# A chunked selective scan: the product with C takes columns 0 to 15 of a chunk, and the products lie with the channel block innermost

## The chip, the cores and the metric

The kernel runs on one core of one Trainium2 chip. The metric is the device time of one execution in microseconds. The engines are TensorE (PE, with its weight loads as PEld), VectorE (DVE), ScalarE (ACT), GpSimd (POOL) and the queue of SyncE (SP), which issues the DMAs.

## The reference, cut to what matters

The network has four residual layers on x of shape (8, 1024, 256): a selective scan block, a mixture of 16 experts, an attention layer and the same mixture again. The change touches the scan. For every channel e (512) and state n (16), and for every time t of 1024:

```
dA = exp(clip(dt[..., None] * A, -10.0, 0.0))
h = dA * h + dt[..., None] * bt[:, None, :] * xt[..., None]
scale = where(|h| > 10.0, 10.0 / |h|, 1)        # norm over n
h = where(t % 16 == 15, h * scale, h)
y = einsum('bn,ben->be', ct, h) + D_param * xt
```

So at each 16th step the state is bounded by its norm, and the bounded state both goes on and enters y. After it y is multiplied by silu(z), projected, normalised and added.

## The kernel before, in words

A tile is 128 consecutive times of one batch entry; there are 64 tiles, and a tile is eight chunks of 16 times (CH = 16, NC = 8). Channels lie on the 128 partitions, in four blocks (EB = 4), with N = 16 states each, so a chunk of the state is 128 partitions by 64 rows of 17 columns: hb[c % 2], whose column 0 is the bounded state that comes in and whose columns 1 to 16 are the times of the chunk.

Per chunk: POOL writes B*u into columns 1 to 16 (inputs, L364). ACT writes the decays exp(dt*A) to PSUM (exponentials, L426). DVE runs the recurrence in place (scan, L980). Then comes the bounding chain: ACT squares column 16 (L432), DVE sums over the states (reduce, L988), ACT makes the factor with a logarithm and an exponential (norms, L438 and L441), and DVE writes the bounded state twice (bound): L997 into column 0 of the other buffer, from which the next scan starts (semaphore st0), and L999 into column 16 of its own buffer (semaphore hs). POOL multiplies columns 1 to 16 by C into prod (product, L356) when hs has come. PE sums the products over n in quarters of a tile (sum_states, L700, 16 transposing matmuls by the identity), ACT copies the sums (L447), PE turns them back into the bank YP, where D*x has been laid before by skip (L741), and DVE multiplies YP by silu(z) (L1154).

The order of each engine is written out in its own step function and is fixed: loops over c from 0 to 7 in which stages of several tiles are interleaved. The letters of the stages are L, F, G (the head of later tiles: norm, projections, convolution, dt, u, decays), S (the scan), B (the rest of the tile before), X and Y (router and experts of tiles further back). Engines meet only by semaphores. On POOL iteration c has product(c-1), inputs(c+1) and, in some chunks, one extra multiply: u in 1 (L373), sz in 4 (L377), xcv in 5 (L380), x1b in 7 (L384). DVE has in each iteration the scan, two expert sums (L1071) for PE's expert pairs (L734), the reduction, other work of the tile, and the bounding.

prod is two buffers of [N, EB, 32 times], one for each quarter in turn. cbc and bbc hold half a tile of C and B, spread over the partitions by DMA; SP reloads them when prodp or bt says that their last reader is done. After the last tile merged runs the attention and the second mixture, 64 slots to a batch entry; twelve pairs of the last two tiles' first mixture are done in the slots LATE of its first batch, all in the one bank G0 (GM); G is (G0, G1), and G1 is also YT, the bank of the state sums.

Of the kernel before, what the change touches and what calls it, by code (L numbers as in the profile page):

```python
# [8 lines left out]
P = 128  # L9
# [20 lines left out]
def build(nc, dram, out):  # L30
# [3 lines left out]
    with ctx:  # L34
# [39 lines left out]
        prod = [sb(f"prod{k}", [P, N, EB, QT]) for k in range(2)]  # L74
# [54 lines left out]
        w_a = prod[0][:].rearrange("p a b c -> p (a b c)").rearrange("p (w k d) -> p w k d", w=4, k=KD)  # L129
        mats = prod[1][:].rearrange("p a b c -> p (a b c)").rearrange("p (m c) -> p m c", c=P)  # L130
# [123 lines left out]
        def chunk_product(c):  # L254

            t0, tq = (c % HC) * CH, (c % QC) * CH
            return (prod[(c // QC) % 2][:].rearrange("p n e t -> p e n t")[:, :, :, tq:tq + CH],
                    hb[c % 2][:].rearrange("p (e n) s -> p e n s", e=EB)[:, :, :, 1:SL],
                    cbc[c // HC][:, :, t0:t0 + CH].rearrange("p (e n) s -> p e n s", e=1).broadcast_to([P, EB, N, CH]))
# [6 lines left out]
        def _(sp):  # L266
# [19 lines left out]
            def step(i, k, stages):  # L286
# [12 lines left out]
                if "G" in stages:  # L299
# [7 lines left out]
                    products_done(sp, i, HC - 1)  # L307
# [38 lines left out]
        def _(g):  # L346
            head_start(g, (M, pool_m))
            TT = nc.gpsimd.tensor_tensor

            def product(i, k, c):  # L350

                g.wait_ge(M["hs"], AHEAD + i * NC + c + 1)
                g.wait_ge(M["cc0" if c < HC else "cc1"], AHEAD + (i + 1) * 16)
                g.wait_ge(M["y"], AHEAD + i * 4 + c // QC - 1)
                dst, states, cc = chunk_product(c)
                TT(dst, states, cc, ALU.mult).then_inc(M["prodp"], 1)  # L356

            def inputs(i, k, c):
# [3 lines left out]
                products_done(g, i if c >= 2 else i - 1, (c - 2) % NC)  # L362
                t0, half = c * CH, c // HC
# [22 lines left out]
            def step(i, k, stages):  # L386
                for c in range(NC):
                    if c == 0 and "B" in stages:
                        product(i - 1, 1 - k, NC - 1)
                    if c > 0 and "S" in stages:  # L390
                        product(i, k, c - 1)
                    if c < NC - 1 and "S" in stages:
                        inputs(i, k, c + 1)
                    extra(i, k, c, stages)
                if "G" in stages:
                    inputs(i + 1, 1 - k, 0)
# [5 lines left out]
        def _(a):  # L402
# [31 lines left out]
            def norms(i, c):  # L434
# [5 lines left out]
                a.wait_ge(M["hs"], AHEAD + q)  # L440
# [248 lines left out]
        def _(pe):  # L689
# [4 lines left out]
            def sum_states(i, h):  # L694

                products_done(pe, i, (h + 1) * QC - 1)
                if h % 2 == 0:
                    pe.wait_ge(M["yt"], AHEAD + i * 2 + h // 2)
                for n in range(N):
                    last = mm(YT[:, h * P:(h + 1) * P], prod[h % 2][:, n, :, :].rearrange("p e t -> p (e t)"), ident[:],  # L700
# [37 lines left out]
            def skip(i, k):  # L738

                for e in range(EB):  # L740
                    mm(YP[:].rearrange("p (h e t) -> p e h t", h=4, e=EB)[:, e, :, :], ddp[:, e, :],  # L741
                       xcv[k][:, e, :].rearrange("p (h t) -> p h t", h=4), start=(e == 0), stop=False)
# [188 lines left out]
            def slot(b, t, p):  # L931
                n = (b - 1) * NT + t
                if b == 0 and t * (X // 2) + p in LATE:
                    m, q = late_pair(t * (X // 2) + p)
                    experts_mm(m, m % 2, q, q + 1, GM)
                if b > 0:
                    experts_mm(n + NTILES, n % 2, p, p + 1, G4 if b == NB else G, fresh=(b in (1, NB) and t == 0))
# [13 lines left out]
        def _(v):  # L951
# [38 lines left out]
            def bound(i, c, top=1.0):  # L990
# [3 lines left out]
                v.wait_ge(M["ne"], AHEAD + q + 1)  # L994
                last = cur[:, :, CH:SL].rearrange("p (e n) s -> p e (n s)", e=EB)
# [3 lines left out]
                STT(last, factor, 1.0, last, ALU.min, ALU.mult).then_inc(M["hs"], 1)  # L999
# [94 lines left out]
            def step(i, k, stages):  # L1094
# [54 lines left out]
                if B:  # L1149
# [4 lines left out]
                    TT(yg[:].rearrange("p e (h t) -> p h e t", h=4), YP[:].rearrange("p (h e t) -> p h e t", h=4, e=EB),  # L1154
                       sz[1 - k][:].rearrange("p e (h t) -> p h e t", h=4), ALU.mult).then_inc(M["yg"], 1)
# [294 lines left out]
```

## Time and profile before

| | us |
|---|---|
| median of 3 runs (lowest, highest) | 4447.61 (4446.76, 4454.78) |
| the profiled execution | 4455.33 |
| its span | 4453.3 |
| PE busy | 3967.3 (89%) |
| DVE busy | 3625.9 (81%) |
| ACT busy | 3121.9 (70%) |
| POOL busy | 2589.8 (58%) |

The scan stage takes the first 27 of 40 equal slices of the span; POOL works in it alone, and after it PE is busy at 90% or more of nearly every slice. Busy time counts instructions, not waits, and start and end of neighbours on one engine overlap by some 0.05 to 0.1 us.

### The profile page before, as it was taken

What the parts mean: (1) busy time and instruction counts of PE and PEld (TensorE: products, weight loads), DVE (VectorE), ACT (ScalarE), POOL (GpSimd) and SP (SyncE); (2) the same over time, 40 slices, a digit from 0 to 9 for tenths busy, and PEclk for the clock granted to TensorE, in tenths of its full rate; (3) what the DMA queues carried; (4) which work ended last, traced back from release to release, by engine and by line L of the source; (5) the groups of instructions that cost most, each with busy time, mean ns of one, the idle gap of its engine ahead of it and who ended that gap; (6) DMA issues with size and microseconds to landing.
All of it is one profiled execution on the core that took longest, in us unless ns stands there. A gap on an engine that the chain in (4) does not pass through costs nothing.

```text
span 4453.3 us, 72570 instructions
## 1 busy us (share of the span) xinstructions
PE 3967.3 (89%) x18752; PEld 2605.9 (59%) x18752; DVE 3625.9 (81%) x9566; ACT 3121.9 (70%) x9232; POOL 2589.8 (58%) x1284
## 2 busy tenths in 40 slices
PE   6788888888888888888888888868999999999999
PEld 5666666666666666666666666634455454454454
DVE  4899999999999999999999999864657666666677
ACT  6899999999999999999999999834333333333321
POOL 4898989889888888898988988840000000000000
PEclk8899999999999999999999999989999999999999
DMA  3111111111111111111111111110000000000000
GB/s 112 53 54 55 54 59 50 59 54 58 54 58 54 58 54 54 54 53 60 50 60 53 58 54 58 53 37 22 7 16 7 16 16 6 16 16 6 7 8 10
DMA packets 91556, 187.43 MB, mean 42 GB/s; under 512 B 16160, under 2 KB 58016, under 8 KB 90912
## 3 DMA queue, kind: packets, MB, share of 16 engines
q1 hardware_dynamic: 91424, 185.92, 13.0%
q8 instruction: 52, 0.85, 0.1%
q14 instruction: 80, 0.66, 0.0%
HBM read 168.05 MB, written 17.83 MB: 42 GB/s over the span
## 4 chain that ended last, share of the span: by engine, by line
PE 39%; issue 22%; POOL 18%; DVE 17%; ACT 3%; DVEq 1%; POOLq 1%; SPq 0%; DMA 0%; ACTq 0%
PE ps L734 21%; POOL prod L356 11%; PE ps L839 5%; DVE macc L1071 4%; POOL hb L364 3%; PE ps L874 3%; PE ps L856 2%; POOL xcv L380 2%; ACT zr L417 2%; DVE sg L1254 2%; POOL u L373 1%; PE ps L833 1%; PE ps L789 1%; PE ps_dA L874 1%; DVE xin L1185 1%
## 5 line engine op out<-in xcount | busy, mean ns | idle before, releaser
L734 PE MATMUL ps<-w_x,mxT 128*128 128x512 f32 x4096 | 1962.3, 607 | 114.6 <-DVE macc L1071 114.6
L1071 DVE SCALAR_TENSOR_TENSOR macc<-ps,gate,macc 128x256 f32<-128x256 f32 x2048 | 978.7, 478 | 492.6 <-PE ps L734 408.8
L980 DVE TENSOR_TENSOR_SCAN hb<-ps_dA,hb 128x1088 f32<-128x1088 f32 x512 | 1240.5, 2423 | 90.1 <-POOL hb L364 77.7
L356 POOL TENSOR_TENSOR prod<-hb,cbc 128x1024 f32<-128x1024 f32 x512 | 1122.5, 2192 | 234.3 <-DVE hb L999 234.0
L364 POOL TENSOR_TENSOR hb<-u,bbc 128x1024 f32<-128x1024 f32 x512 | 1203.1, 2350 | 75.1 <-POOL prod L356 70.9
L417 ACT ACTIVATE zr<-dt,aneg 128x128 f32<-128x128 f32 x4096 | 1239.8, 387 | 0.0
L734 PEld LDWEIGHTS ps<-w_x,mxT 128*128 128x128 f32 x4096 | 736.0, 194 | 819.6 <-issue 601.4
L700 PE MATMUL ps<-ident,prod 128*128 128x128 f32 x4096 | 554.6, 295 | 12.8 <-POOL prod L356 9.6
L700 PEld LDWEIGHTS ps<-ident,prod 128*128 128x128 f32 x4096 | 513.0, 153 | 25.3 <-POOL prod L356 22.5
L426 ACT ACTIVATE ps_dA<-zr 128x1024 f32<-128x1024 f32 x512 | 518.2, 1012 | 0.0
L477 ACT ACTIVATE ex<-lgt,ms 128x16 f32<-128x16 f32 x128 | 39.1, 305 | 357.9 <-DVE ms L1019 357.9
L432 ACT ACTIVATE sq<-hb 128x64 f32<-128x64 f32 x512 | 158.3, 309 | 174.2 <-DVE hb L980 172.0
L811 PEld LDWEIGHTS ps<-xin,dcw 128*128 128x128 f32 x2048 | 247.3, 198 | 40.7 <-DVE xin L1185 25.3
L811 PE MATMUL ps<-xin,dcw 128*128 128x128 f32 x2048 | 248.4, 281 | 11.0 <-DVE xin L1185 11.0
L839 PE MATMUL ps<-xcv,w_dt 128*128 128x128 f32 x2048 | 253.2, 283 | 0.0
L839 PEld LDWEIGHTS ps<-xcv,w_dt 128*128 128x128 f32 x2048 | 241.0, 197 | 13.5 <-issue 13.5
L773 PE MATMUL ps<-ident,xn 128*128 128x128 f32 x128 | 31.8, 336 | 157.3 <-ACT xn L520 157.3
L833 PE MATMUL ps<-xcv,w_xp 128*32 128x128 f32 x512 | 70.9, 284 | 103.4 <-POOL xcv L380 103.4
L789 PE MATMUL ps<-xnT,w_in 128*128 128x128 f32 x1024 | 150.6, 310 | 3.9 <-ACT xnT L542 3.9
L789 PEld LDWEIGHTS ps<-xnT,w_in 128*128 128x128 f32 x1024 | 145.8, 227 | 4.7 <-ACT xnT L542 3.4
L997 DVE SCALAR_TENSOR_TENSOR hb<-ps_dA,hb 128x64 f32<-128x64 f32 x480 | 125.9, 262 | 24.9 <-ACT ps_dA L441 21.9
L833 PEld LDWEIGHTS ps<-xcv,w_xp 128*32 128x32 f32 x512 | 52.2, 112 | 154.0 <-POOL xcv L380 150.3
(197 smaller groups left out, 5102.8 us busy)
## 6 DMA issues: line engine op xcount, KB each, us to landing
bbc<-bcd SPq DMA_DIRECT2D x128, 512.0 KB, 3.7
cbc<-bcd SPq DMA_DIRECT2D x128, 512.0 KB, 3.8
xt<-in_x SPq DMA_DIRECT2D x128, 128.0 KB, 3.7
x2d<-macc SPq DMA_DIRECT2D x64, 128.0 KB, 1.7
out_dram<-macc SPq DMA_DIRECT2D x64, 128.0 KB, 1.7
w_x<-in_w_x SPq DMA_DIRECT2D x1, 4096.0 KB, 14.8
hb<-x2d SPq DMA_DIRECT2D x32, 128.0 KB, 2.3
sz<-x2d SPq DMA_DIRECT2D x16, 128.0 KB, 2.2
```

Source lines behind the costliest of these rows:

```text
L356: TT(dst, states, cc, ALU.mult).then_inc(M["prodp"], 1)
L364: TT(hb[c % 2][:].rearrange("p (e n) s -> p e n s", e=EB)[:, :, :, 1:SL], u[k][:, :, t0:t0 + CH].rearrange("p e (n s) -> p e n s", n=1).br ...
L417: last = act(zr[k][:, s, :], dt[:, s // N, :], ACT.Relu, bias=10.0, scale=aneg[:, s:s + 1])
L426: act(dA3[:, :, 1:SL], zr[k][:, :, c * CH:(c + 1) * CH], ACT.Exp, bias=-10.0).then_inc(M["dA"], 1)
L700: last = mm(YT[:, h * P:(h + 1) * P], prod[h % 2][:, n, :, :].rearrange("p e t -> p (e t)"), ident[:], start=(h % 2 == 0 and n == 0), stop ...
L734: last = mm(banks[p % len(banks)][:], mxT[k][:, j, :], w_x[:, j, p * 512:(p + 1) * 512], start=(j == 0), stop=(j == KD - 1))
L789: last = mm(F0[:, m * P:(m + 1) * P], w_in[:, j, m * P:(m + 1) * P], xnT[:, j, :], start=(j == 0), stop=(j == KD - 1))
L811: last = mm(F0[:, e * P:(e + 1) * P], dcw[:, e * TAPS + t, :], xin[:, e, t:t + P], start=(t == 0), stop=(t == TAPS - 1))
L839: last = mm(F0[:, m * P:(m + 1) * P], w_dt[:, e, m * P:(m + 1) * P], xcv[k][:, e, :], start=(e == 0), stop=(e == EB - 1))
L874: last = mm(QUAD[s % 4][:], w_a[:, w, kk, j * P:(j + 1) * P], xTa[:, kk, g * TG:(g + 1) * TG], start=(kk == 0), stop=(kk == KD - 1))
L980: V.tensor_tensor_scan(states, dA, states, 0.0, ALU.mult, ALU.add).then_inc(M["scan"], 1)
L1071: STT(macc[k][:], banks[(e // 2) % len(banks)][:, (e % 2) * D:(e % 2 + 1) * D], gate[k][:, e:e + 1], macc[k][:], ALU.mult, ALU.add).then_i ...
```

## The change

The product takes columns 0 to 15 of a chunk instead of 1 to 16. Column 0 is the bounded state of the chunk before, so the column that needs the second bounding form is read from the next chunk's buffer instead. The product waits for the scan; only the last column of a tile (last_product) waits for the second form, which is left in chunk 7 alone. In chunk 0 the product takes columns 1 to 15, and in chunk 4 it is cut in two, since column 0 belongs to the first half of C. On POOL iteration c now has product(c), the extra, and inputs(c+2). These inputs wait for the squares and the first form of chunk c, and the first form waits for product c-1, which reads the column that it writes. prod is one buffer of [N, 64 times, EB]; a quarter's sums wait for product 2, 4, 6 or the last one. The late expert pairs alternate between G0 and G1.

```
-        prod = [sb(f"prod{k}", [P, N, EB, QT]) for k in range(2)]
+        prod = sb("prod", [P, N, HT, EB])
...
+        QUARTER_ENDS = (2, 4, 6, 7)
+        def states_product(c, s0, s1):
+            t0 = c * CH + s0 - 1
+            half, at, w = t0 // HT, t0 % HT, s1 - s0
+            return (prod[:].rearrange("p n t e -> p e n t")[:, :, :, at:at + w],
+                    hb[c % 2][:].rearrange("p (e n) s -> p e n s", e=EB)[:, :, :, s0:s1],
+                    cbc[half][:, :, at:at + w].rearrange("p (e n) s -> p e n s", e=1).broadcast_to([P, EB, N, w]))
...                                                          # SP
-                    products_done(sp, i, HC - 1)
+                    products_done(sp, i, HC)
...                                                          # POOL, product
-                g.wait_ge(M["hs"], AHEAD + i * NC + c + 1)
-                g.wait_ge(M["cc0" if c < HC else "cc1"], AHEAD + (i + 1) * 16)
+                g.wait_ge(M["scan"], AHEAD + i * NC + c + 1)
                 g.wait_ge(M["y"], AHEAD + i * 4 + c // QC - 1)
-                dst, states, cc = chunk_product(c)
-                TT(dst, states, cc, ALU.mult).then_inc(M["prodp"], 1)
+                if c == 0:
+                    g.wait_ge(M["cc0"], AHEAD + (i + 1) * 16)
+                    multiply(c, 1, CH).then_inc(M["prodp"], 1)
+                elif c == HC:
+                    multiply(c, 0, 1)
+                    g.wait_ge(M["cc1"], AHEAD + (i + 1) * 16)
+                    multiply(c, 1, CH).then_inc(M["prodp"], 1)
+                elif c < NC - 1:
+                    multiply(c, 0, CH).then_inc(M["prodp"], 1)
+                else:
+                    multiply(c, 0, CH)
+            def last_product(i):
+                g.wait_ge(M["hs"], AHEAD + i + 1)
+                multiply(NC - 1, CH, SL).then_inc(M["prodp"], 1)
...                                                          # POOL, inputs
+                g.wait_ge(M["sq"], AHEAD + i * NC + c - 1)
+                g.wait_ge(M["st0"], AHEAD + i * NC + c - 1)
...                                                          # POOL, step
-                    if c == 0 and "B" in stages:
-                        product(i - 1, 1 - k, NC - 1)
-                    if c > 0 and "S" in stages:
-                        product(i, k, c - 1)
-                    if c < NC - 1 and "S" in stages:
-                        inputs(i, k, c + 1)
+                    if "S" in stages:
+                        product(i, k, c)
                     extra(i, k, c, stages)
-                if "G" in stages:
-                    inputs(i + 1, 1 - k, 0)
+                    if c == NC - 1 and "S" in stages:
+                        last_product(i)
+                    if c < NC - 2 and "S" in stages:
+                        inputs(i, k, c + 2)
+                    if c >= NC - 2 and "G" in stages:
+                        inputs(i + 1, 1 - k, c + 2 - NC)
...                                                          # ACT, norms
-                a.wait_ge(M["hs"], AHEAD + q)
+                a.wait_ge(M["st0"], AHEAD + q)
+                if c == 0:
+                    a.wait_ge(M["hs"], AHEAD + i)
...                                                          # PE
-                products_done(pe, i, (h + 1) * QC - 1)
+                products_done(pe, i, QUARTER_ENDS[h])
-                    last = mm(YT[:, h * P:(h + 1) * P], prod[h % 2][:, n, :, :].rearrange("p e t -> p (e t)"), ident[:],
+                    last = mm(YT[:, h * P:(h + 1) * P], prod[:, n, h % 2 * QT:(h % 2 + 1) * QT, :].rearrange("p t e -> p (t e)"), ident[:],
-                    mm(YP[:].rearrange("p (h e t) -> p e h t", h=4, e=EB)[:, e, :, :], ddp[:, e, :],
-                       xcv[k][:, e, :].rearrange("p (h t) -> p h t", h=4), start=(e == 0), stop=False)
+                    mm(YP[:].rearrange("p (t e) -> p e t", e=EB)[:, e, :], ddp[:, e, :], xcv[k][:, e, :], start=(e == 0),
+                       stop=False)
...
-                    experts_mm(m, m % 2, q, q + 1, GM)
+                    if t * (X // 2) + p == LATE[0]:
+                        pe.wait_ge(R["ac"], AHEAD + m * (X + 1) + 2 * q + 1)
+                        pe.wait_ge(M["yt"], AHEAD + NTILES * 2)
+                    experts_mm(m, m % 2, q, q + 1, G)
...                                                          # DVE, bound
+                products_done(v, i, c - 1)
                 STT(nxt[:, :, 0:1].rearrange("p (e n) s -> p e (n s)", e=EB), factor, top, last, ALU.min, ALU.mult)\
                     .then_inc(M["st0"], 1)
-                STT(last, factor, 1.0, last, ALU.min, ALU.mult).then_inc(M["hs"], 1)
+                if c == NC - 1:
+                    STT(last, factor, 1.0, last, ALU.min, ALU.mult).then_inc(M["hs"], 1)
...
-                    TT(yg[:].rearrange("p e (h t) -> p h e t", h=4), YP[:].rearrange("p (h e t) -> p h e t", h=4, e=EB),
-                       sz[1 - k][:].rearrange("p e (h t) -> p h e t", h=4), ALU.mult).then_inc(M["yg"], 1)
+                    TT(yg[:], YP[:].rearrange("p (t e) -> p e t", e=EB), sz[1 - k][:], ALU.mult).then_inc(M["yg"], 1)
...
-                    expert_sums(m, m % 2, 2 * q, 2 * q + 2, GM)
+                    expert_sums(m, m % 2, 2 * q, 2 * q + 2, G)
```

## Rows read from the trace of the kernel before

**Rows 1.** Windows: busy us and count of each engine in 400 to 2800 us.
```profile
400.00:2800.00 2400.00, 2098.10 (x12091) 1562.34 (x12090) 2222.74 (x5363) 2192.03 (x6684) 2146.72 (x1061) 0.96 0.17 56
```

**Rows 2.** POOL by line, whole run: busy us, mean ns, idle before and its releasers.
```profile
L364 POOL TENSOR_TENSOR hb<-u,bbc 128x1024 f32<-128x1024 f32 x512 | 1203.1, 2350 | 75.1 <-POOL prod L356 70.9 <-PE ps L700 0.2
L356 POOL TENSOR_TENSOR prod<-hb,cbc 128x1024 f32<-128x1024 f32 x512 | 1122.5, 2192 | 234.3 <-DVE hb L999 234.0
L377 POOL TENSOR_TENSOR sz<-zt,sg 128x512 f32<-128x512 f32 x64 | 81.8, 1278 | 6.3 <-ACT sg L564 6.3
L384 POOL TENSOR_TENSOR x1b<-oo,xt 128x256 f32<-128x256 f32 x64 | 47.2, 738 | 13.9 <-DVE oo L1193 13.9
```

**Rows 3.** Timeline of DVE, chunks 0 to 5: start us, us, instruction, idle before.
```profile
1415.55 2.42 DVE L980 TENSOR_TENSOR_SCAN hb<-ps_dA,hb 128x1088 f32<-128x1088 f32 x1 [0.17 <-issue]
...
1420.63 0.26 DVE L997 SCALAR_TENSOR_TENSOR hb<-ps_dA,hb 128x64 f32<-128x64 f32 x1
...
1421.03 2.42 DVE L980 TENSOR_TENSOR_SCAN hb<-ps_dA,hb 128x1088 f32<-128x1088 f32 x1
...
1425.46 0.27 DVE L997 SCALAR_TENSOR_TENSOR hb<-ps_dA,hb 128x64 f32<-128x64 f32 x1 [0.22 <-ACT ps_dA L441]
...
1426.05 2.42 DVE L980 TENSOR_TENSOR_SCAN hb<-ps_dA,hb 128x1088 f32<-128x1088 f32 x1
...
1429.81 0.42 DVE L1163 TENSOR_TENSOR oo<-oo,ps 128x256 f32<-128x256 f32 x1 [0.31 <-PE ps L796]
1430.26 0.43 DVE L1165 BATCH_NORM_STATS2 st<-oo 128x6 f32<-128x256 f32 x1
...
1431.13 0.26 DVE L997 SCALAR_TENSOR_TENSOR hb<-ps_dA,hb 128x64 f32<-128x64 f32 x1
...
1431.95 2.42 DVE L980 TENSOR_TENSOR_SCAN hb<-ps_dA,hb 128x1088 f32<-128x1088 f32 x1 [0.40 <-POOL hb L364]
...
1438.00 2.42 DVE L980 TENSOR_TENSOR_SCAN hb<-ps_dA,hb 128x1088 f32<-128x1088 f32 x1
...
1442.98 2.42 DVE L980 TENSOR_TENSOR_SCAN hb<-ps_dA,hb 128x1088 f32<-128x1088 f32 x1
```

**Rows 4.** The same timeline, from the end of chunk 5 to the next tile.
```profile
1448.09 0.25 DVE L997 SCALAR_TENSOR_TENSOR hb<-ps_dA,hb 128x64 f32<-128x64 f32 x1
...
1448.84 2.42 DVE L980 TENSOR_TENSOR_SCAN hb<-ps_dA,hb 128x1088 f32<-128x1088 f32 x1 [0.33 <-POOL hb L364]
...
1454.04 0.21 DVE L1245 TENSOR_SCALAR sc<-mv,sc 128x1 f32<-128x1 f32 x1
1454.72 2.42 DVE L980 TENSOR_TENSOR_SCAN hb<-ps_dA,hb 128x1088 f32<-128x1088 f32 x1 [0.47 <-POOL hb L364]
...
1460.33 2.42 DVE L980 TENSOR_TENSOR_SCAN hb<-ps_dA,hb 128x1088 f32<-128x1088 f32 x1
```

**Rows 5.** Timeline of ACT: the squares of chunks 4 and 5.
```profile
1440.45 0.32 ACT L432 ACTIVATE sq<-hb 128x64 f32<-128x64 f32 x1 [0.93 <-DVE hb L980]
...
1446.01 0.30 ACT L432 ACTIVATE sq<-hb 128x64 f32<-128x64 f32 x1
```

**Rows 6.** The same timeline: the squares of chunks 6 and 7.
```profile
1451.56 0.30 ACT L432 ACTIVATE sq<-hb 128x64 f32<-128x64 f32 x1
...
1457.65 0.30 ACT L432 ACTIVATE sq<-hb 128x64 f32<-128x64 f32 x1
```

**Rows 7.** ACT by line, 1000 to 2000 us: busy us, mean ns, idle before.
```profile
L432 ACT ACTIVATE sq<-hb 128x64 f32<-128x64 f32 x177 | 54.7, 309 | 52.0 <-DVE hb L980 51.3
L438 ACT ACTIVATE nrl<-nrs 128x4 f32<-128x4 f32 x177 | 34.7, 196 | 6.3 <-DVE nrs L988 5.5
...
L560 ACT ACTIVATE sg<-zt 128x512 f32<-128x512 f32 x22 | 13.9, 631 | 0.3
```

**Rows 8.** Timeline of PE: the sums of the first quarter.
```profile
1432.66 1.91 PE L700 MATMUL ps<-ident,prod 128*128 128x128 f32 x16
```

**Rows 9.** Timeline of PE in the slots of the late expert pairs: one of them.
```profile
3068.24 1.98 PE L734 MATMUL ps<-w_x,mxT 128*128 128x512 f32 x4 [1.17 <-DVE macc L1071]
```

More of the change, by code:

```diff
@@ L128, in build @@
         kv = big[1][:, 2 * AW:4 * AW].rearrange("p (t d) -> p t d", t=NT)
-        w_a = prod[0][:].rearrange("p a b c -> p (a b c)").rearrange("p (w k d) -> p w k d", w=4, k=KD)
-        mats = prod[1][:].rearrange("p a b c -> p (a b c)").rearrange("p (m c) -> p m c", c=P)
+        products = prod[:].rearrange("p a b c -> p (a b c)")
+        w_a = products[:, 0:4 * KD * D].rearrange("p (w k d) -> p w k d", w=4, k=KD)
+        mats = products[:, 4 * KD * D:].rearrange("p (m c) -> p m c", c=P)
         ac = sb("ac", [P, 50])
@@ L252, in flat @@
             return t[:].rearrange("p a b -> p (a b)")
[L254 to L259, printed above, removed]
+        QUARTER_ENDS = (2, 4, 6, 7)
[5 more added lines that the diff above has]
+                    cbc[half][:, :, at:at + w].rearrange("p (e n) s -> p e n s", e=1).broadcast_to([P, EB, N, w]))
         block = ctx.enter_context(nc.Block())
@@ L348, in _, with multiply @@
             TT = nc.gpsimd.tensor_tensor
+            def multiply(c, s0, s1):
+                dst, states, cc = states_product(c, s0, s1)
+                return TT(dst, states, cc, ALU.mult)
             def product(i, k, c):
-                g.wait_ge(M["hs"], AHEAD + i * NC + c + 1)
-                g.wait_ge(M["cc0" if c < HC else "cc1"], AHEAD + (i + 1) * 16)
+                g.wait_ge(M["scan"], AHEAD + i * NC + c + 1)
                 g.wait_ge(M["y"], AHEAD + i * 4 + c // QC - 1)
-                dst, states, cc = chunk_product(c)
-                TT(dst, states, cc, ALU.mult).then_inc(M["prodp"], 1)
+                if c == 0:
[12 more added lines that the diff above has]
+                multiply(NC - 1, CH, SL).then_inc(M["prodp"], 1)
             def inputs(i, k, c):
@@ L934, in slot @@
                     m, q = late_pair(t * (X // 2) + p)
-                    experts_mm(m, m % 2, q, q + 1, GM)
+                    if t * (X // 2) + p == LATE[0]:
+                        pe.wait_ge(R["ac"], AHEAD + m * (X + 1) + 2 * q + 1)
+                        pe.wait_ge(M["yt"], AHEAD + NTILES * 2)
+                    experts_mm(m, m % 2, q, q + 1, G)
                 if b > 0:
-                    experts_mm(n + NTILES, n % 2, p, p + 1, G4 if b == NB else G, fresh=(b in (1, NB) and t == 0))
+                    experts_mm(n + NTILES, n % 2, p, p + 1, G4 if b == NB else G, fresh=(b == NB and t == 0))
                 m = routed(b, t)
```

## The prediction

> **What bounds the kernel now.** I first read the busy time of each engine in a long stretch of the scan stage [rows 1]: DVE works 2223 of 2400 us, ACT 2192, POOL 2147, PE 2098. Three engines are at 89 to 93%, so none bounds alone, and the question is which of them ends each wait. A tile is eight chunks. On POOL each chunk has one B*u product (2.35 us, "inputs") and one product with C (2.19 us), and each tile has three 1.28 us multiplies and one of 0.74 [rows 2].
>
> Then the DVE timeline of one tile [rows 3, 4]. I count from its first scan, S0 = 1415.55. The scans start at S1 5.48, S2 10.50, S3 16.40, S4 22.45, S5 27.43, S6 33.29, S7 39.17, and the next tile at 44.78. The reader is to see three kinds of chunk. In chunks 0, 3 and 4 the scan follows the bounding form (L997) after 0.40 (1420.63 to 1421.03; below I leave the 1400 out) with no idle time: DVE itself is late, and the second form (L999) stands between. After chunks 1, 2, 5 and 6 the scan is held for its inputs: the row of S3 shows 0.40 "<-POOL hb", those of S6 and S7 0.33 and 0.47, and S2 comes 0.59 after its bounding form where chunk 0 shows 0.40. In chunk 1 the bounding form itself waits 0.22 for ACT's factor.
>
> Last the squares of ACT [rows 5, 6], the head of the bounding chain. The one of chunk 4 waited 0.93 us for its scan. Those of chunks 5, 6 and 7 (30.46, 36.01, 42.10) waited for nothing: 5.56, 5.55 and 6.09 us apart, they follow ACT's own work, while their scans had ended 0.61, 0.30 and 0.51 earlier (start + 2.42). ACT is full from chunk 4 to chunk 7. That decides how much of the edit is seen.
>
> **The change, part by part.**
>
> *The second bounding form* goes in 7 of 8 chunks. It lasts 0.26 but moves the next start by about 0.2, as neighbours overlap; and it hid the wait of the scan for the first form's result. A DVE instruction that waits for its neighbour starts 0.03 after its end (29.81 + 0.42 to 30.26) [rows 3]. So form to scan goes from 0.40 to 0.26 + 0.04 = 0.30, a gain of 0.10 and not 0.26. The bounds are 0.41 (the 0.15 that some neighbours show, no gain here) and 0.22 (0.18 gain); I take 0.30 by the nearest row.
>
> *The order on POOL.* The product starts when its scan ends, not when the bounding is over (some 3 us later), and the inputs of chunk c+2 follow it, once bounding c is done. From scan end: product 2.2, an extra multiply 1.2 in three chunks (0.7 in a fourth), inputs 2.3: they are ready 4.7 to 6 us after the end of scan c (up to 1.2 us more where POOL is behind after chunks 1, 4 and 5), and scan c+2 starts about 8 after it. So inputs 6 are ready near 30.1 (S6 at 32.2), inputs 7 near 35.8 (S7 at 38.1). The waits for POOL in rows 3 and 4 go. The new waits are covered: the bounding form of c waits for product c-1, over 1.5 us done; inputs wait for squares and form, which stand before the next scan.
>
> *One tile walked again*, from S0 = 0:
> - S1: 5.48 - 0.10 = 5.38.
> - The squares of chunk 1 are held by ACT's stretch of chunk 0, which hangs on S0, not S1: the form stays at 9.91, S2 = 9.91 + 0.30 = 10.21.
> - Chunk 2 waits 0.31 for PE's output product (L1163) [rows 3]. PE got there from ACT's copy in chunk 0, so the form stays at 15.58 and S3 = 15.88 (before 16.40).
> - Chunks 3 and 4 are DVE's own: S4 = 15.88 + 6.05 - 0.09 = 21.84, S5 = 21.84 + 4.98 - 0.09 = 26.73 (before 27.43).
> - Squares 4 at 21.84 + 2.45 = 24.29. Now ACT's stretches count: squares 5 at 29.85 (its scan ended at 29.15), form 2.08 later at 31.93 (48.09 - 46.01), S6 = 32.23 (before 33.29).
> - Squares 6 at 29.85 + 5.55 = 35.40. The last small instruction before scan 7 (L1245) follows squares 6 by 2.48 and lasts 0.21: S7 = 35.40 + 2.48 + 0.24 = 38.12 (before 39.17).
> - Squares 7 at 35.40 + 6.09 = 41.49, 0.95 after its scan. The next tile's scan stands 2.68 behind it (57.65 to 60.33), the reduction on DVE waits for it in order, and chunk 7 keeps both forms: 44.17 (before 44.78).
>
> So 1.05 us is gained up to S7, and 0.4 is given back to ACT in chunk 7. Net 0.61 a tile, times 64: **39 us**. Bounds: with form to scan at 0.41 the walk gives 0.4 a tile (25 us); where ACT did not hold anything, every term would count, chunk by chunk from 0 to 6 what stands now between form and scan less 0.30 (in chunk 6 the 0.47 of waiting and 0.16 of the second form): 0.10 + 0.29 + 0.52 + 0.09 + 0.09 + 0.45 + 0.63 = 2.17 a tile (139 us).
>
> *The layout of the products.* POOL now writes with 16 bytes between neighbours instead of 4; the element count is the same (15+48+1+15+48+1 = 128 columns), in two instructions more. From 0.74 for 256 and 1.28 for 512 elements the fixed part is 0.20 [rows 2]: +0.4 us a tile. No POOL instruction in the trace writes with a stride inside its runs. The nearest row is ACT's square, which reads one word in 68 bytes: 64 elements 309 ns against 196 for 4, that is 1.88 ns each, where a dense one costs (631 - 196)/508 = 0.86 [rows 7]. From below the cost is 0 (a gain is excluded, as a dense write can't be slower per word). From above, added fully, 1.02 ns times 1024 = 1.05 us a product. I take 0: even 1.88 ns is under the 1.94 ns that POOL spends on each element anyway ((2192 - 203)/1024), so a slower write can lie beside it.
>
> The Trainium skill (GPSIMD Engine Reference, Performance pitfalls for Q7 kernels) says that reads with over 8 bytes between elements cost about one cycle more for each. It speaks of reads, no run here shows it for writes; if it held for this write, an estimate by that page is 0.85 us a product, and the sum would end near 4650 instead (between the two prices of the first rival below).
>
> How much POOL can bear: it idles (2400 - 2147)/2400 of 45 us = 4.75 a tile. Off go 0.4 for the two instructions and some 0.8 for the 0.15 to 0.2 between a product and the inputs that wait for it: 3.55 are left at today's pace, 2.9 at the new one. So the write is hidden up to 2.9/8 = 0.36 us a product, and the kernel is as fast as before at 0.44.
>
> *Costed at nothing.* The gating multiply on DVE (L1154) reads PSUM with a stride: 0 to 0.5 us (512 times 1.02 ns); it lies before chunk 1's form, where 0.22 is idle, and the rest ends in chunk 2's wait for PE. PE's skip product writes PSUM with a stride; behind it PE waits for macc anyway. PE's sums of a quarter wait for product 2, 4 and 6 instead of 1, 3 and 5: these end near 15.5, 26.7 and 37.9, and PE comes to the first at 17.1 [rows 8], to the others as far behind. SP's loads: cbc[0] waits for product 4 (26.7), needed near 46; cbc[1] and bbc come no later than now. The last product waits for both forms of chunk 7; behind it stand inputs 1 of the next tile, ready 2.7 us later, 2.7 before their scan.
>
> *Behind the scan stage.* The last product is 0.34 instead of 2.19: 2 us off the path, once. Twelve late expert pairs get two banks instead of one. PE waited 1.17 us for DVE before such a pair [rows 9], seven times in a row or nearly (0.59 to 1.45, 7 in all); DVE and ACT take part of it back. 0 to 7, taken 5.
>
> **Sum.** 39 + 2 + 5 = 46 us off the profiled execution, 4455.3 (span 4453.3): 4409. That execution lies 7.7 above the median of the runs, 4447.6, so I predict 4401.
>
> **Rivals.**
> - *POOL's strided write is not hidden (slower).* One mechanism: each of 512 products takes d longer, and POOL becomes the bound from d = 0.36. For: no dense write is left, and POOL has the least room. Against: 1.94 ns an element is slow already. Slower than before from d = 0.44; at 1.05 it is 8 x 0.61 = 4.9 us a tile, +312, 4750; at 0.6, 82 us over the time before, less 7: 4523. Chance 0.24.
> - *Nothing to measure.* d near 0.4, or ACT and the dependent scan take back the rest (0.41 form to scan and another 0.3 in chunk 7). 4440 to 4456, taken 4445. Against: waits for POOL of 0.33 to 0.47 in three chunks do go. Chance 0.10.
> - *The whole 2.17 counts.* ACT's stretches from chunk 4 to 7 shrink or slip without holding DVE. 4447.6 - 139 - 7 = 4302. Against: those stretches show no idle time. Chance 0.08.
> - *The forecast.* Own range 4375 to 4430. Chance 0.58.
>
> **How the numbers follow.** 0.2% (9 us) is about what a measurement of this kernel can tell from no change. Faster 0.58 + 0.08 = 0.66, same 0.10, slower 0.24. The range reaches from 4350 to 4560: the large gain (0.08) and write costs over 0.66 us (about 0.10) are left out.
>
> **What would show it.** Of the POOL line of the product: mean near 2.1 to 2.2 and busy as now; over 2.55 and the forecast is dead. "DVE hb L980 <- POOL" gone from the waits. POOL's wait moves from L999 to the scan. Squares of chunks 5 to 7 late after their scans by 0.7 to 0.95. Tile pitch 0.6 shorter. If the scans of chunk 6 and 7 still wait for POOL, my order on POOL is wrong; if squares wait for DVE in chunks 5 to 7, my ACT bound is.

## The result and the profile after

The changed kernel takes 4582.62 us (median of 4 runs, 4581.36 to 4583.35), the kernel before beside it 4447.18 (4440.49 to 4454.78): ratio 1.0304, interval 1.0286 to 1.0322. It is 135 us slower; 4401 was forecast, and the time lies outside the range. The profiled span is 4581.5 us.

The page first: busy times of the engines, and one queue of its list (packets, MB, share). In the kernel before that queue shows 80 packets.

```profile
PE 3999.4 (87%) x18752; PEld 2627.6 (57%) x18752; DVE 3613.3 (79%) x9118; ACT 3120.5 (68%) x9232; POOL 2649.5 (58%) x1412
q14 instruction: 217, 1.77, 0.1%
```

The long window answers to [rows 1]; the two of 5 us (length, busy and count of PE, PEld, DVE, ACT, POOL, granted clock, DMA share, GB/s) lie at a place told below.

```profile
400.00:2800.00 2400.00, 2026.81 (x11469) 1510.31 (x11468) 2095.47 (x4725) 2073.68 (x6325) 2079.14 (x1106) 0.94 0.16 53
1475.00:1480.00 5.00, 3.06 (x17) 3.06 (x18) 1.32 (x3) 1.77 (x4) 2.76 (x2) 0.74 0.67 213
1485.00:1490.00 5.00, 2.71 (x13) 2.48 (x14) 4.54 (x7) 4.95 (x17) 4.87 (x3) 0.77 0.00 0
```

All four engines do less in the same 2400 us than in [rows 1]: no engine has become the bound, something holds all of them. POOL by line and shape, against [rows 2]:

```profile
L388 POOL TENSOR_TENSOR hb<-u,bbc 128x1024 f32<-128x1024 f32 x512 | 1204.4, 2352 | 212.4 <-DVE hb L1027 166.7 <-POOL prod L357 34.0 <-issue 11.5
L357 POOL TENSOR_TENSOR prod<-hb,cbc 128x1024 f32<-128x1024 f32 x384 | 867.3, 2259 | 13.4 <-DVE hb L1009 2.1
L357 POOL TENSOR_TENSOR prod<-hb,cbc 128x960 f32<-128x960 f32 x128 | 271.0, 2117 | 90.4 <-DVE hb L1009 90.4
L357 POOL TENSOR_TENSOR prod<-hb,cbc 128x64 f32<-128x64 f32 x128 | 54.7, 428 | 73.3 <-DVE hb L1030 61.4 <-DVE hb L1009 10.9
```

A whole product lasts 2.26 us instead of 2.19: the strided write, my rival for the slower side, is not the cause (it needed 0.44 more a product to be slower than before).

The lost time is in one place of every second tile. DVE's timeline there (start, duration, instruction, idle time before it and its releaser), against [rows 3, 4]:

```profile
1468.68 2.42 DVE L1009 TENSOR_TENSOR_SCAN hb<-ps_dA,hb 128x1088 f32<-128x1088 f32 x1
...
1475.38 0.27 DVE L1030 SCALAR_TENSOR_TENSOR hb<-ps_dA,hb 128x64 f32<-128x64 f32 x1
1479.19 2.42 DVE L1009 TENSOR_TENSOR_SCAN hb<-ps_dA,hb 128x1088 f32<-128x1088 f32 x1 [3.54 <-POOL hb L388]
...
1489.49 2.42 DVE L1009 TENSOR_TENSOR_SCAN hb<-ps_dA,hb 128x1088 f32<-128x1088 f32 x1
1493.38 1.00 DVE L1102 SCALAR_TENSOR_TENSOR macc<-ps,gate,macc 128x256 f32<-128x256 f32 x2 [1.46 <-PE ps L760]
...
1496.76 2.42 DVE L1009 TENSOR_TENSOR_SCAN hb<-ps_dA,hb 128x1088 f32<-128x1088 f32 x1
```

The first scan of the tile comes 10.51 us after the scan before it, and the releaser named is "POOL hb L388". POOL's timeline says otherwise: the inputs that this scan reads end at 1471.51, before DVE's idle time begins; those of 1476.46 are for the scan after it.

```profile
1469.16 2.35 POOL L388 TENSOR_TENSOR hb<-u,bbc 128x1024 f32<-128x1024 f32 x1 [0.29 <-POOL prod L357]
...
1476.46 2.34 POOL L388 TENSOR_TENSOR hb<-u,bbc 128x1024 f32<-128x1024 f32 x1 [0.31 <-POOL prod L357]
```

Nothing that the profile shows releases the scan. The place is where DVE's loop over pairs of tiles (28 rounds) turns back; of the 27 turns each has this gap, and no other place has it. The DMA list of 450 to 2750 us has, in the kernel after:

```profile
DMA packets 52344, 121.33 MB, mean 53 GB/s; under 512 B 9216, under 2 KB 27648, under 8 KB 52224
q14 instruction: 120, 0.98, 0.1%
```

and in the kernel before, with every packet under 8 KB and no instruction queue at all:

```profile
DMA packets 55344, 127.35 MB, mean 55 GB/s; under 512 B 9776, under 2 KB 29360, under 8 KB 55344
```

So instructions are fetched again while the loop runs: 120 packets of 8192 B in 24 rounds, five in a round. The wait is seen on PE too, some us later:

```profile
1482.56 1.98 PE L760 MATMUL ps<-w_x,mxT 128*128 128x512 f32 x4 [1.94 <-DVE macc L1102]
1487.17 0.44 PE L734 MATMUL ps<-ident,yT 128*128 128x128 f32 x2 [2.62 <-ACT yT L473]
...
1488.21 3.32 PE L815 MATMUL ps<-xnT,w_in 128*128 128x128 f32 x16
```

PE runs dry twice, its granted clock is 0.74 and 0.77 in the two windows above (between its levels of 2.4 and 1.2 GHz), and the 16 matmuls of L815 take 3.32 us, where in the kernel before they take 1.95. Then DVE waits 1.46 us for PE's expert pair, and the scan of chunk 3 comes 7.27 after that of chunk 2. So one fetch costs twice: at the turn, and again in chunk 2 of the next tile.

Medians of the time from each scan to the next (chunk 0 to 1, and so on; last column the mean tile), over tiles 8 to 55, even and odd tiles apart; each follows from the scan rows of the DVE timeline. "Forecast" is the walk of the prediction, which took one even tile; e1 and e9 are told below. Chunk 2 has two lengths, and a median can fall between them: before, it is 6.96 in every second even tile and 5.90 in the others, so 6.39 is no tile's length.

| kernel | 0 | 1 | 2 | 3 | 4 | 5 | 6 | 7 | tile |
|---|---|---|---|---|---|---|---|---|---|
| before, even | 5.48 | 5.00 | 6.39 | 6.05 | 4.98 | 5.84 | 5.89 | 5.61 | 45.22 |
| before, odd | 5.46 | 5.02 | 5.90 | 6.00 | 4.99 | 5.84 | 5.89 | 6.04 | |
| forecast | 5.38 | 4.83 | 5.67 | 5.96 | 4.89 | 5.50 | 5.89 | 6.05 | 44.17 |
| after, even | 5.48 | 4.83 | 7.30 | 6.05 | 4.98 | 5.73 | 5.68 | 6.28 | 47.79 |
| after, odd | 5.92 | 4.46 | 5.56 | 6.40 | 4.98 | 5.73 | 5.68 | 10.54 | |
| e1, even | 5.63 | 4.69 | 5.69 | 6.05 | 4.99 | 5.86 | 5.56 | 6.28 | 45.51 |
| e1, odd | 5.92 | 4.46 | 5.57 | 6.38 | 4.98 | 5.73 | 5.69 | 6.80 | |
| e9, even | 5.45 | 4.87 | 5.69 | 5.70 | 4.98 | 5.65 | 5.48 | 6.31 | 44.37 |
| e9, odd | 5.54 | 4.77 | 5.64 | 5.65 | 4.98 | 5.52 | 5.60 | 6.45 | |

### The profile page after: what moved, and what is told of

Its sections match the earlier page's. It is cut to its first block and busy times, and to the rows that moved or that the text cites. A ratio compares the mean times of both kernels' runs of the same rounds, so it can differ in the third digit from the quotient of the medians.

```text
span 4581.5 us, 73219 instructions
## 1 busy us (share of the span) xinstructions
PE 3999.4 (87%) x18752; PEld 2627.6 (57%) x18752; DVE 3613.3 (79%) x9118; ACT 3120.5 (68%) x9232; POOL 2649.5 (58%) x1412
## 5 line engine op out<-in xcount | busy, mean ns | idle before, releaser
L388 POOL TENSOR_TENSOR hb<-u,bbc 128x1024 f32<-128x1024 f32 x512 | 1204.4, 2352 | 212.4 <-DVE hb L1027 166.7
L357 POOL TENSOR_TENSOR prod<-hb,cbc 128x1024 f32<-128x1024 f32 (+2 forms) x640 | 1190.0, 1864 | 177.2 <-DVE hb L1009 103.4
L815 PE MATMUL ps<-xnT,w_in 128*128 128x128 f32 x1024 | 171.1, 338 | 3.5 <-ACT xnT L568 3.5
L815 PEld LDWEIGHTS ps<-xnT,w_in 128*128 128x128 f32 x1024 | 167.9, 257 | 4.5 <-ACT xnT L568 3.1
```

Source lines behind the costliest of these rows:

```text
L357: return TT(dst, states, cc, ALU.mult)
L388: TT(hb[c % 2][:].rearrange("p (e n) s -> p e n s", e=EB)[:, :, :, 1:SL], u[k][:, :, t0:t0 + CH].rearrange("p e (n s) -> p e n s", n=1).br ...
L815: last = mm(F0[:, m * P:(m + 1) * P], w_in[:, j, m * P:(m + 1) * P], xnT[:, j, :], start=(j == 0), stop=(j == KD - 1))
```

## The experiments

DVE's program, as the kernel writes it, has 584 instructions ahead of the loop and 369 in it before; after, 588 and 371: 14 second forms are gone from the loop, and 16 waits for the product have come. Packets of 8192 B hold 128 instructions if one is 64 B long. The theory: the loop runs without fetches while it lies within a few whole blocks, and when it touches one more, it is fetched again in each round. Then it is the place of the loop that counts, and instructions ahead of it can shift it. The rival: the new order itself makes DVE wait.

**e1_short_head.** The changed kernel, with ten of DVE's semaphore increments (the head start that lets the first tiles pass) behind the loop instead of ahead of it.

```
-            head_start(v, (M, dve_m), (R, dve_x), (A, dve_a))
+            head_start(v, (M, dve_m), (R, dve_x), (A, dve_a[:14]))
...
             pipeline(v, step)
+            head_start(v, (A, dve_a[14:]))
```

> The changed kernel with 10 of DVE's semaphore increments moved from ahead of its tile loop to behind it, so that the loop's code starts 10 instructions earlier. Nothing in the loop differs. Theory (DVE's loop code now crosses into one more block of instruction memory and is fetched anew in each of the 28 rounds, 5 blocks of 8192 bytes each): no instruction packets inside the loop, no 3.5 us wait of the first scan, two tiles in 89.3 us instead of 95.5, in all 4390 to 4415 us. Rival (the strided write of the products, 2.26 instead of 2.19 us, or the new waits cause the loss): 4575 to 4590, as the changed kernel.

4460.63 us, ratio 1.0028 (1.0018 to 1.0037) to the kernel before's 4448.67. No instruction packets from 450 to 2750 us:

```profile
DMA packets 55200, 126.82 MB, mean 55 GB/s; under 512 B 9760, under 2 KB 29344, under 8 KB 55200
```

122 of the 135 us are the place of ten instructions that do nothing for the work, and nothing in the loop differs. But it is 4460, not the 4390 to 4415 that my forecast asked for: the rest of the change, without the fetches, is 12 us slower than before, and not 46 faster.

**e2_before_pad6** is the reverse: the kernel before with six increments more ahead of the loop.

```
             v.wait_ge(s_zero, 3)
+            for _ in range(6):
+                settle()
             pipeline(v, step)
```

> The kernel before, with 6 semaphore increments of DVE added ahead of its tile loop; the loop is unchanged. Theory of the instruction blocks: the loop now crosses into one more block, 5 packets of 8192 bytes in each of 28 rounds, 5 to 6 us more in each: 4590 to 4620 us. Rival (loss lies in the change itself): 4447 us, since 6 increments cost well under 1 us.

4567.88 us, ratio 1.0273 (1.0257 to 1.0289): 119 us for six increments, or 4.4 us for each of the 27 turns, where 5 to 6 were expected. DMA list of 450 to 2750 us, and what ended DVE's idle time ahead of the scans (us, times):

```profile
DMA packets 53238, 123.30 MB, mean 54 GB/s; under 512 B 9355, under 2 KB 28157, under 8 KB 53117
q14 instruction: 121, 0.99, 0.1%
```

```profile
  issue: 84.6, 22
  POOL hb L364: 63.5, 137
```

Here the same wait is named "issue", with 84.6 / 22 = 3.85 us each, and its after-effect in chunk 2 is there too (7.10 in even tiles). This is the changed kernel's loss, in a kernel without the change.

**e3_before_pad120**: the same edit with 120 increments.

> The kernel before, with 120 semaphore increments of DVE added ahead of its tile loop. If blocks are 128 instructions (8192 bytes at 64 each), the loop starts 8 instructions earlier in its block than before and stays in three: no instruction packets in the loop, 4445 to 4460 us. Rival (more code ahead of the loop costs by itself, or the blocks are larger): 4590 us or more.

4458.19 us, 1.0022 (1.0012 to 1.0031), and again no packet of 8 KB in the loop:

```profile
DMA packets 55390, 127.47 MB, mean 55 GB/s; under 512 B 9792, under 2 KB 29376, under 8 KB 55390
```

Twenty times the increments, and the loss is gone but for some 10 us, which its tiles don't show (mean 45.17). They lie ahead of the loop: the first scan starts at 73.46 us instead of 63.71, so the 120 increments cost about 10 us by being executed. For the loop it is the place within a block that counts, not the number.

**e10_short_head4**: the changed kernel with four increments behind the loop (dve_a[:20] and dve_a[20:] in e1's edit), so that its loop begins where that of the kernel before does.

> The changed kernel with only 4 of DVE's semaphore increments moved from ahead of the tile loop to behind it: the loop starts exactly where it starts in the kernel before and has 371 instructions where that has 369. If the start in the block of 128 was 14 or 15 before, the two more are enough to cross: 5 instruction packets a round, 4570 to 4590 us. If it was 10 to 13, the loop stays in three blocks and the four instructions ahead of the loop did it: 4455 to 4465.

4581.49 us (one run), and the 120 packets are back. With the same start, 369 instructions fit and 371 don't.

Two sizes of block explain these starts (against the kernel before: free are 0 and +120 with 369 and -6 with 371; +6 with 369, 0 and +4 with 371 fetch): blocks of 128 with three of them in reach and the kernel before beginning at the 14th or 15th place of one, or blocks of 256 with two in reach and a beginning 128 places further. **e13_before_pad150**, e3's edit with 150 increments, tells them apart.

> The kernel before with 150 increments on DVE ahead of its loop (e2 had 6, e3 120). Two sizes of block explain the starts tried so far (-6, 0, +4, +6, +120). Theory A, blocks of 128 instructions of which a loop may touch three: it runs free if it begins at places 0 to 15 of a block; with the kernel before at place 14 or 15, +150 begins at 36 or 37, so the loop touches a fourth block: instruction packets in the loop, about five a round, and 4570 to 4600 us. Theory B, blocks of 256 of which it may touch two: the kernel before then begins at place 142 or 143, +150 at 36 or 37 of the next block, and 369 instructions end at 405 of 512: no packets in the loop, 4450 to 4470 us.

4576.28 us, 1.0288 (1.0270 to 1.0305), with the packets back (about 13 of the 128 us are the 150 increments themselves: the first scan starts at 77.10):

```profile
DMA packets 52633, 122.39 MB, mean 53 GB/s; under 512 B 9248, under 2 KB 27680, under 8 KB 52512
q14 instruction: 121, 0.99, 0.1%
```

```profile
  issue: 93.9, 24
  POOL hb L364: 52.3, 129
```

That is the same pair of views as of e2: 24 rounds, 24 waits, 93.9 / 24 = 3.91 us each.

Theory A: blocks of 128 instructions, and a loop of 369 that touches three of them is free. The beginning at the 14th or 15th place was fitted to these runs, not read from anything. Blocks of 64 with six in reach would fit the same starts; that it is 128 rests on the packets of 8192 B. Why it is five packets a round, when the loop touches four blocks, stays open.

The Trainium skill (Runtime: NRT & Kernel Launch, Instruction fetch mechanics) says that instructions are refilled in blocks of 16 KiB, 256 instructions, and that a taken branch whose target lies outside the current window of two pages waits for a fetch. In kind the runs agree. The sizes are those of theory B, by which e13 would have run at 4450 to 4470; here the measurement decides for the smaller block, as do the packets of 8192 B and their odd number, five a round.

**e7_layout_alone**: the kernel before with only the layout of the products changed (prod, sums, skip, gating).

```
-        prod = [sb(f"prod{k}", [P, N, EB, QT]) for k in range(2)]
+        prod = sb("prod", [P, N, HT, EB])
...
-            return (prod[(c // QC) % 2][:].rearrange("p n e t -> p e n t")[:, :, :, tq:tq + CH],
+            return (prod[:].rearrange("p n t e -> p e n t")[:, :, :, t0:t0 + CH],
```

> The kernel before with the layout alone: products as [state, 64 times, channel block], the sums, the skip product and the gating multiply read and write accordingly; order, forms and waits as before, DVE's code as long as before. In the changed kernel POOL's product took 2.26 us instead of 2.19. Theory (a small cost on POOL, which three scans in eight wait for in this order): product 2.26, 0.2 to 0.5 us a tile, 4458 to 4480 us. Rival (the layout is free, or the strided write is dearer in this order): 4445 to 4452, or over 4500.

4444.55 us, 0.9997 (0.9988 to 1.0006): no difference, as the first of the two rivals said. The product costs 17 ns more than in [rows 2]:

```profile
L357 POOL TENSOR_TENSOR prod<-hb,cbc 128x1024 f32<-128x1024 f32 x512 | 1131.2, 2209 | 220.9 <-DVE hb L1000 216.3 <-PE ps L701 4.5
```

Two small things cancel in this sum. Leaving out the long chunks 2, the medians of its chunks add up to 44.87 in even tiles and 45.25 in odd ones, against 44.75 and 45.15 before: 0.11 a tile, 7 us. But in the profiled execution only 3 tiles have the long chunk 2 instead of 15, which is worth 13 us (why it comes so seldom here is not known).

**e8_one_late_bank**: e1 with the twelve late pairs back in the one bank (GM for G, and the two waits ahead of the first pair out).

> The changed kernel with DVE's code ahead of the loop shortened by 10 (as e1_short_head, 4461 us), and the twelve late expert pairs in one bank again. If the second bank is worth what PE's waits in front of those pairs showed: 5 to 10 us over e1_short_head, 4466 to 4471. Rival (other work fills the gap): 4461.

4463.82 us, between the two expectations, against e1's 4460.63 on another chip. Two banks are worth 3 us by these medians, 5 by the ratios to the kernel before beside each (1.0039 and 1.0028), and 7 by the profiled spans behind the last scan (1507.2 and 1500.4); the scan stages of the two are alike.

**e4_short_head_decays**: e1, with ACT's exponentials of a tile spread otherwise over the chunks, fewer of them in the late ones.

```
-        DECAYS = (0, 6, 13, 19, 30, 37, 50, 64, 64)
+        DECAYS = (0, 6, 14, 20, 34, 41, 53, 64, 64)
```

> As the first of these, and ACT's 64 decay instructions lie otherwise over the chunks: 6, 8, 6, 14, 7, 12, 11 instead of 6, 7, 6, 11, 7, 13, 14. Theory (with the fetch gone ACT's work in chunks 4 to 7 holds the reductions of DVE, which gives back 0.4 to 1 us a tile): 15 to 40 us under the first of these. Rival (DVE's own work is the bound): no difference, within 5 us.

4436.49 us, 0.9971 (0.9960 to 0.9983): 24 us under e1, as expected. The reduction's idle time for ACT falls by 20 us. Not all of the gain is ACT's: the long chunk 2 comes in 12 tiles instead of 19, some 5 us. DVE's reductions in e1 and in e4 (busy, mean ns, idle before):

```profile
L1017 DVE TENSOR_REDUCE nrs<-sq 128x4 f32<-128x64 f32 x512 | 107.4, 210 | 47.2 <-ACT sq L456 46.8 <-issue 0.3
```

```profile
L1017 DVE TENSOR_REDUCE nrs<-sq 128x4 f32<-128x64 f32 x512 | 106.3, 208 | 26.9 <-ACT sq L456 26.5 <-issue 0.3
```

**e12_before_decays**: the same DECAYS in the kernel before.

> The kernel before with the decays of ACT spread as in e4_short_head_decays, and nothing else. Theory (in the kernel before POOL ends the waits of three scans in eight, so lighter ACT stretches there buy little; they pay only once the order on POOL is changed): 4435 to 4447 us. Rival (ACT's stretches held the kernel before just as much): 4415 to 4425, the same 24 us as there.

4451.12 us, 1.0012 (1.0003 to 1.0021): no gain, even a little over the theory's range. There the reduction waited only 11.7 us in all, and the scans of chunks 5 and 6 were held by POOL [rows 4] as much as by ACT. ACT's stretches hold the chunks only once POOL's order has been changed, as the walk had it.

**e9_fillers**: e4, with three DVE instructions moved from ahead of the bounding form to behind it (L1175 in chunk 0, L1223 in 3, L1251 in 5). Nothing else differs.

```
-                    STT(oo[:], oo[:], sc[:, 12:13], be_row[:], ALU.mult, ALU.add).then_inc(M["o4"], 1)
                 end(3)
+                    STT(oo[:], oo[:], sc[:, 12:13], be_row[:], ALU.mult, ALU.add).then_inc(M["o4"], 1)
```

> As e4_short_head_decays (4436 us), with one DVE instruction each moved from ahead of the bounding form to behind it, between form and scan: L1175 in chunk 0, L1223 in chunk 3, the statistics L1251 in chunk 5. Theory (form to scan stayed at 0.39 us where 0.30 was forecast, because the scan waits for the form's result; the moved work hides in it): 0.2 us in each of the three chunks where nothing else holds, 4405 to 4428 us. Rival (an instruction with two inputs in SBUF is held while POOL works, and POOL starts its inputs at the form): L1175 over 1.5 us, 4450 or more.

4394.38 us, 0.9880 (0.9865 to 0.9895): 42 us under e4 (40 by the ratios, as e4 ran on another chip), more than expected, and faster than both kernels. Where the 0.2 us in each of three chunks came out is another matter: in the means of tiles 8 to 55 chunk 0 is 0.38 shorter than in e4 and chunk 1 0.34 longer, chunk 3 is 0.58 shorter and chunk 5 0.21. So chunk 0 gave nothing. Chunk 3 gave more than the hidden instruction, since L1220, which stays where it was, falls from 697 to 549 ns beside POOL (e11 tells why). The same three moves were not tried in the kernel before, so their gain can't be credited to the new order. In e1 a scan comes 0.39 after its form though nothing stands between them:

```profile
1491.46 0.26 DVE L1027 SCALAR_TENSOR_TENSOR hb<-ps_dA,hb 128x64 f32<-128x64 f32 x1
1491.85 2.42 DVE L1009 TENSOR_TENSOR_SCAN hb<-ps_dA,hb 128x1088 f32<-128x1088 f32 x1
```

In e9 0.57 and 0.50, with an instruction of 0.48 and one of 0.42 between them:

```profile
1412.74 0.26 DVE L1027 SCALAR_TENSOR_TENSOR hb<-ps_dA,hb 128x64 f32<-128x64 f32 x1
1412.91 0.48 DVE L1224 SCALAR_TENSOR_TENSOR oo<-oo,sc,be_row 128x256 f32<-128x256 f32 x1
1413.31 2.42 DVE L1009 TENSOR_TENSOR_SCAN hb<-ps_dA,hb 128x1088 f32<-128x1088 f32 x1
...
1423.44 0.26 DVE L1027 SCALAR_TENSOR_TENSOR hb<-ps_dA,hb 128x64 f32<-128x64 f32 x1
1423.61 0.42 DVE L1252 BATCH_NORM_STATS2 st<-xt 128x6 f32<-128x256 f32 x1
1423.94 2.40 DVE L1009 TENSOR_TENSOR_SCAN hb<-ps_dA,hb 128x1088 f32<-128x1088 f32 x1
```

The scan waits for the semaphore st0, which the form increments, and can't start before 0.39 from the form's start. The second form of the kernel before (0.26) had stood in that gap nearly for nothing: form to scan was 0.40 with it and is 0.39 without.

**e11_row_in_psum**: e9, with the row ob_row, which L1175 adds, copied once to free columns of PSUM. In the changed order L1175 costs 837 ns instead of 625, and the theory is that an instruction with two inputs in SBUF is held by POOL. One place in e1, where POOL's product ends at 1469.85 and the DVE instruction at 1470.12, and where another ends 0.27 after POOL's 1485.76; first POOL's rows, then DVE's:

```profile
1467.73 2.12 POOL L357 TENSOR_TENSOR prod<-hb,cbc 128x960 f32<-128x960 f32 x1
...
1483.51 2.25 POOL L357 TENSOR_TENSOR prod<-hb,cbc 128x1024 f32<-128x1024 f32 x1
```

```profile
1468.98 1.14 DVE L1175 SCALAR_TENSOR_TENSOR oo<-xt,r1b,ob_row 128x256 f32<-128x256 f32 x1
...
1485.14 0.89 DVE L1220 SCALAR_TENSOR_TENSOR oo<-oo,mv,ga_row 128x256 f32<-128x256 f32 x1
```

```
+            V.tensor_copy(ob_ps, ob_row[:])
...
-            STT(oo[:], xt[1][:], r1b[1 - k][:], ob_row[:], ALU.mult, ALU.add)
+            STT(oo[:], xt[1][:], r1b[1 - k][:], ob_ps, ALU.mult, ALU.add)
```

> As e9_fillers, and the bias row that L1175 adds lies in PSUM (copied there once), so this instruction has one input in SBUF. Theory (DVE instructions with both inputs in SBUF are held by POOL's; L1175 went from 0.59 to 0.89 us with the change): L1175 at 0.42 to 0.49 us whatever POOL does, up to 0.4 us a tile, 0 to 25 us under e9_fillers. Rival (its length comes from something else): the same length as in e9_fillers and the same time.

4393.05 us, 0.9879 (0.9864 to 0.9894), no difference to e9. The instruction in e9 and in e11:

```profile
L1176 DVE SCALAR_TENSOR_TENSOR oo<-xt,r1b,ob_row 128x256 f32<-128x256 f32 x64 | 54.8, 856 | 0.2 <-issue 0.2
```

```profile
L1179 DVE SCALAR_TENSOR_TENSOR oo<-xt,r1b,ps_dA 128x256 f32<-128x256 f32 x64 | 30.5, 477 | 0.0
```

856 to 477 ns: the duration was POOL's doing. In e1 the two rows above are no exception: all 88 of L1175 and L1220 that start with more than 0.25 us of a POOL instruction still to run end 0.26 to 0.29 us after it. The time doesn't follow: in even tiles chunk 0 shortens to 5.19 and chunk 1 grows to 5.12 (from 5.45 and 4.87), since the reduction of chunk 1 then waits 0.24 us longer for ACT's squares. The Trainium skill (SBUF — State Buffer, Who interferes with whom) says that a DVE instruction with two SBUF inputs contends with a GpSimd instruction that reads SBUF, and that the port pair which they share is locked by one of them at a time. The trace agrees for the DVE instruction that comes second.

## Why the prediction was wrong

**The step that is missing.** The prediction counted what each engine executes, waits for and moves, and not the length and place of its code. No rival had it. In the diff a round of DVE's loop has 16 waits more and 14 forms less; the prediction costed the waits as covered. As two instructions more in a loop of 369, with four more ahead of it, they were 122 of 135 us. The 80 instruction packets of the page before, none of them in the loop, could only have told that the loop then fitted, not by how little.

**Form to scan from 0.40 to 0.30.** It stays at 0.39 (e1, e9). I took the price of a dependent instruction from a wait for a neighbour's end (0.03), whose waiter is not the scan. The prediction's own bound for this (0.41: 25 us instead of 39) takes 14 us off the gain.

**"The waits for POOL in rows 3 and 4 go."** Right. In e1 the scans' idle time for POOL is 0.3 us where it was 77.7 before (the first row is of the kernel before, the others of e1):

```profile
L980 DVE TENSOR_TENSOR_SCAN hb<-ps_dA,hb 128x1088 f32<-128x1088 f32 x512 | 1240.5, 2423 | 90.1 <-POOL hb L364 77.7 <-issue 5.2 <-ACT ps_dA L426 0.2
L1009 DVE TENSOR_TENSOR_SCAN hb<-ps_dA,hb 128x1088 f32<-128x1088 f32 x512 | 1240.6, 2423 | 56.7 <-issue 5.4 <-POOL hb L388 0.3
L1220 DVE SCALAR_TENSOR_TENSOR oo<-oo,mv,ga_row 128x256 f32<-128x256 f32 x64 | 40.2, 628 | 2.3
L1092 DVE TENSOR_TENSOR selp<-ex,rest 128x16 f32<-128x16 f32 x128 | 38.1, 297 | 0.0
```

**What moving POOL does to DVE was costed at nothing.** Because the products now follow the scans, POOL runs beside other DVE instructions than before. L1175 costs 17.1 us more in all (57.1 in e1, 40.0 before), L1220 7.9 (before 504 ns), L1092 13.2 (before 194 ns). Not all of it is on the path. L1175 is in chunk 0, and what it takes there chunk 1 gives back: the two together are 10.32 and 10.38 in e1 where they were 10.48 before. L1220 makes chunk 3 of odd tiles 6.38 instead of 6.00. L1092 stands right ahead of the last forms of the tile and is on it in every tile; first POOL's row, which ends at 1463.97, then DVE's, which ends at 1464.00:

```profile
1463.25 0.72 POOL L408 TENSOR_TENSOR x1b<-oo,xt 128x256 f32<-128x256 f32 x1
1463.61 0.39 DVE L1092 TENSOR_TENSOR selp<-ex,rest 128x16 f32<-128x16 f32 x1
```

**"ACT is full from chunk 4 to chunk 7" and gives back part of the gain.** Right in kind (e4 against e12), and in chunk 7 in size too. The reduction there starts 3.75 after its scan instead of 3.31, 0.44 later, and 0.44 was forecast (6.05 - 5.61). That chunk 7 costs 6.28 in even tiles is this and the 0.2 of L1092. Odd tiles, of which the prediction walked none, stood at 6.04 already before and come to 6.80. In e9 they are still 6.31 and 6.45; there it is L1094, the next multiply, that costs 406 ns instead of 234, 22 us in all.

**Layout at nothing, bounds 0 to 1.05 us a product.** Right in the whole time: e7. In the changed kernel the mean is 67 ns more than in [rows 2] instead of 17; the skip product and the gating multiply cost nothing that the time shows. The small instructions were mis-sized: 428 ns for 64 elements, where the prediction had 0.34. POOL has room for it.

**Behind the scan stage: 2 and 5.** The span after the last scan's start falls from 4453.3 - 2942.0 = 1511.3 to 1500.4 in e1 (4455.0 - 2954.6), 11 where 7 were forecast; e8 gives the two banks 3 to 7 of them. The last product alone wasn't tried. So all that went wrong in e1 is in the scan stage: its last scan starts 12.6 us later than before, not 39 earlier.

**What it adds up to.** e1's tile is 45.51 where the forecast leaves 45.22 - 0.61 = 44.61: 58 us over 64 tiles. By the means of tiles 8 to 55 they lie 10 in chunks 0 and 1, 8 in chunk 2, 14 in chunk 3, 6 in chunk 4, 2 in chunks 5 and 6 and 17 in chunk 7. Of the terms above, form to scan makes 14, L1220 up to 8 and L1092 13. One part was no step of mine: TensorE's granted clock. In some tiles PE stands idle for 2 us or more in chunk 1 (2.6 in the first of the two tiles below), its granted clock falls to 0.57, between its levels of 2.4 and 1.2 GHz, and the scan of chunk 3 waits behind it. Two tiles of e1, one with the fall and one without, and the window (as above) of the first:

```profile
1154.52 3.01 PE L815 MATMUL ps<-xnT,w_in 128*128 128x128 f32 x16
1200.25 1.95 PE L815 MATMUL ps<-xnT,w_in 128*128 128x128 f32 x16
1155.00:1157.00 2.00, 2.00 (x12) 2.00 (x12) 1.65 (x3) 1.95 (x9) 2.00 (x2) 0.57 0.00 0
```

Chunk 2 is then 6.9 us long instead of 5.6: 19 tiles and 25 us in e1, 15 tiles and 16 us before, so 9 of the 58 us. That leaves some 14 us without a cause. Of these terms only L1175's (e11), ACT's (e4) and what hides behind the form (e9) were tried by a run; L1220's, L1092's and the clock's are read from e1's trace.

## What to carry to other kernels

Where a large loop runs on an engine, look at the instruction queue's packets inside the loop: if there are none, the loop fits, and an edit that adds instructions to it or ahead of it may end that; try it by moving idle instructions ahead of the loop, before reasoning on the change. An idle time for which the named releaser had ended long before, or "issue", at the place where a loop turns back, was a fetch here. When an instruction is taken out from between a producer and its reader on the same engine, count only what is above the producer's own latency, and put other work in the gap; here three moved lines gave some 40 us, nearly all of it in two of the three chunks, and the new order on POOL without them no gain. Before moving work on POOL, look which DVE instructions with two SBUF inputs it will then run beside. And walk a tile of each kind: here odd and even tiles differ by 0.4 us.

## What the runs showed of the hardware

- DVE's loop back over the edge of what stays loaded costs 3.6 to 4.1 us of idle DVE on average (after, e2, e13, e10) and five packets of 8192 B, and with what follows on PE 122 / 27 = 4.5 us a turn.
- A semaphore increment that DVE executes ahead of the loop costs some 80 to 90 ns: the first scan comes 9.75 us later for 120 of them (e3) and 13.4 later for 150 (e13). The first scans of the other runs differ by up to 5 us among themselves, so this is rough.
- A scan that waits for the bounding form just ahead of it starts 0.39 us after the form's start, 0.13 after its end; an independent instruction starts 0.17 after the form's start. The 0.13 is of this pair: L1165, which waits for L1163, starts 0.03 after its end [rows 3]. Whether result, semaphore or the scan's other waits make the difference was not tried.
- A DVE instruction of 128x256 with two SBUF inputs that starts beside a POOL product with over 0.25 us to run ends 0.26 to 0.29 us after it (1.14 and 0.89 us instead of 0.48), and with one input in PSUM it doesn't (477 ns). One of 128x16 (L1092) ends 0.03 after POOL's.
- POOL's writes with 16 bytes between neighbours cost 17 ns in 2192 (e7), 67 in the changed order.
- After PE stood idle for 2.6 us its granted clock was 0.58 and 0.57 in the next two windows of 2 us, and 16 matmuls of 128 columns took 3.01 us instead of 1.95 (e1, 1153 to 1157 us).
